# Edge loop of a four-layer GNN on one core: the sum, maximum and product of the group ahead placed between the one-hots of the two item chains

## The reference, cut to what matters

```
g      = leaky_relu(xl[src] + xr[dst] + edge_attr @ W_e, 0.2)
logits = einsum('ehc,hc->eh', g, att)
amax   = segment_max(logits, dst);  ex = exp(logits - amax[dst])
out    = segment_sum(xl[src] * ex / (segment_sum(ex, dst)[dst] + 1e-16), dst) + bias
```

## Time and profile before

| | |
|---|---|
| median of 3 runs | 6465.83 us |
| profiled execution, its own time | 6478.12 us |
| its span | 6476.2 us |
| mean granted TensorE clock | 0.731 |
| PE, DVE, ACT, POOL busy, share of the span | 78%, 46%, 28%, 60% |
| first and last start of a gather of the edge loop | 438.3 and 2843.4 us |

### The profile page before, as it was taken

The page is one execution under the profiler, slowest core; times in us unless marked ns, Lnnn a source line. Parts: engine busy times, 40 slices in busy tenths (PEclk is TensorE's granted clock), DMA queues, the critical chain, the costliest instruction groups (busy, mean ns, idle before and its releaser), DMA issues. The chain is left out here.

```text
span 6476.2 us, 113947 instructions
## 1 busy us (share of the span) xinstructions
PE 5047.6 (78%) x35178; PEld 4313.9 (67%) x35178; DVE 2978.9 (46%) x3937; ACT 1845.2 (28%) x3914; POOL 3856.6 (60%) x3427
## 2 busy tenths in 40 slices
PE   2328888888888888870799967888787788885899
PEld 2315665666555665550799967778777777774899
DVE  7657877777777777755422131111111111112321
ACT  0015555555555455530000002222222222221100
POOL 5747887888888888853000017777777777776000
PEclk9667888888888888865899975555555555555799
DMA  9325555555555555531799946666667666664598
GB/s 358 83 79 141 154 144 148 155 153 144 149 150 152 142 152 153 155 97 36 259 366 366 364 143 215 202 206 201 201 204 208 207 205 204 205 209 122 228 397 329
DMA packets 622991, 1260.53 MB, mean 195 GB/s; under 512 B 131705, under 2 KB 431290, under 8 KB 597220
## 3 DMA queue, kind: packets, MB, share of 16 engines
q10 hardware_dynamic: 217740, 649.85, 31.5%
q1 hardware_dynamic: 295768, 492.49, 21.2%
q0 software_dynamic: 109184, 115.05, 8.6%
HBM read 923.85 MB, written 490.51 MB: 218 GB/s over the span
## 5 line engine op out<-in xcount | busy, mean ns | idle before, releaser
L697 POOL DMA_INDIRECT att_gl<-tab_l,top_zero x1568 | 1928.4, 1230 | 488.5 <-issue 475.6
L1177 POOL DMA_INDIRECT sum_gl<-tab_l,top_zero x1568 | 1547.4, 987 | 517.5 <-issue 477.6
L930 ACT ACTIVATE att_acc<-att_pc 128x392 bf16<-128x392 f32 x2352 | 1088.0, 497 | 1326.7 <-PE att_pc L713 1201.3
L710 PE MATMUL att_pc<-att_ohl,att_ohv 128*128 128x392 bf16 x2352 | 867.5, 369 | 260.9 <-DVE att_ohl L810 260.8
L1105 PE MATMUL sum_pm<-sum_msg,sum_S 128*128 128x64 f32 x3136 | 683.6, 413 | 388.8 <-ACT sum_msg L1145 388.8
L713 PE MATMUL att_pc<-att_acc,att_ohv 128*128 128x392 bf16 x2352 | 861.4, 366 | 116.2 <-ACT att_acc L930 112.7
L1105 PEld LDWEIGHTS sum_pm<-sum_msg,sum_S 128*128 128x128 f32 x3136 | 657.8, 321 | 421.6 <-ACT sum_msg L1145 219.1
L1075 DVE TENSOR_TENSOR sum_t<-sum_pb,sum_gl 128x512 f32<-128x512 f32 x196 | 135.6, 692 | 1659.3 <-DMA sum_gl<-tab_l,top_zero 1276.0
L1087 PE MATMUL sum_pb<-sum_wbs,sum_ea 64*128 64x64 f32 x3136 | 694.5, 419 | 28.1 <-DMA sum_ea<-in_ea64T 28.1
L729 PEld LDWEIGHTS att_pl<-att_xe,att_S 128*128 128x128 f32 x3136 | 603.9, 218 | 161.2 <-issue 138.7
L1087 PEld LDWEIGHTS sum_pb<-sum_wbs,sum_ea 64*128 64x128 f32 x3136 | 676.1, 329 | 39.7 <-DMA sum_ea<-in_ea64T 28.3
(11 more groups left out here) (373 smaller groups left out, 5268.7 us busy)
## 6 DMA issues: line engine op xcount, KB each, us to landing
A<-att_acc SPq DMA_DIRECT2D x2352, 98.0 KB
l_a<-A SPq DMA_DIRECT2D x147, 1568.0 KB, 9.3
att_dall<-in_dst ACTq DMA_DIRECT2D x224, 448.0 KB
sum_dall<-in_dst ACTq DMA_DIRECT2D x196, 512.0 KB, 7.1
hop_at<-AT SPq DMA_DIRECT2D x56, 1568.0 KB
sum_a<-A ACTq DMA_DIRECT2D x49, 1568.0 KB, 10.2
AT<-sum_at ACTq DMA_DIRECT2D x49, 1568.0 KB, 6.4
l_at<-AT SPq DMA_DIRECT2D x42, 1568.0 KB
```

The lines of the kernel that those rows point to most:

```text
L697: nc.gpsimd.indirect_dma_start(out=gl[s][:, k * GQ + j, :], out_offset=None, in_=g.tab_l, in_offset=bass.IndirectOffsetOnAxis(ap=g.ix[:, c ...
L710: nc.tensor.matmul(pc[c][m % 2][:, 0:LO], ohv[c][h][:, m, :, 0], ohl[c][h][:, m // 2, :, m % 2], start=True, stop=False)
L930: nc.scalar.activation(acc[c][n % CR][:, :], pc[c][m % 2][:, 0:LO], ACT.Copy).then_inc(s_acc[c], 1)
L1177: nc.gpsimd.indirect_dma_start(out=gl[n % RB][:, j, :], out_offset=None, in_=g.tab_l, in_offset=bass.IndirectOffsetOnAxis(ap=g.ix[:, c:c + ...
```

## The change

`items` makes ohl ahead of ohv. `logits` keeps its first three operations; the fourth, with the signal `s_L` behind it, becomes `head_sums`. VectorE's slot is then: `same`, `items` of chain 0, softmax or messages where due, `logits` of the group ahead, `items` of chain 1, `head_sums` of the group ahead. No other engine's program changes.

```diff
                     if not known(i, 1) or t >= 2:
                         dve.wait_ge(s_mm[c], i * (CB * CJ) + (at0[t - 1] if t >= 2 else (-SLOTS[SL - 1], 0)[t]))
+                    v.tensor_tensor(ohl[c][h][:, 0:w // 2, :, :], spread(c_lo2[:, :, :].unsqueeze(1), [P, w // 2, LO, 2]),
+                                    spread(g.lo[:, bass.ds(n0, w)].rearrange("p (j two) -> p j two", two=2).unsqueeze(2),
+                                           [P, w // 2, LO, 2]), ALU.is_equal).then_inc(s_oh[c], 1)
                     v.tensor_tensor(ohv[c][h][:, 0:w, :, :], spread(c_row2[:, :, :].unsqueeze(1), [P, w, P, 2]),
                                     spread(g.vals[:, bass.ds(n0, w), :].unsqueeze(2), [P, w, P, 2]), ALU.is_equal)\
                         .then_inc(s_oh[c], 1)
-                    v.tensor_tensor(ohl[c][h][:, 0:w // 2, :, :], spread(c_lo2[:, :, :].unsqueeze(1), [P, w // 2, LO, 2]),
...
                     step(v.tensor_tensor(t2[:, :, :], t2[:, :, :], spread(att[:, :].unsqueeze(1), [P, GQ, D]),
                                          ALU.mult))
+
+                def head_sums(n, b, s, k):
+                    step = InOrder(dve, s_step, n * 3 + (b * 4 + 6))
                     step(v.tensor_reduce(L[s][:, :, k * GQ:(k + 1) * GQ].rearrange("p h g -> p g h"),
...
                         same(i, t)
-                        for c in range(CH):
-                            items(i, t, c)
+                        items(i, t, 0)
                         if k == 1 and known(b, 1):
                             v.memset(apart[:, :], 0.0).then_inc(s_step, 4)
                         elif k == 1:
                             softmax(b - 1, i * SL + (t - 1))
                         if k == 2 and not known(b, 1):
                             messages(b - 1, 1 - s)
+                        n = i * SL + (t - 1)
                         if t:
-                            logits(i, i * SL + (t - 1), b if k else b - 1, s if k else 1 - s, (k - 1) % NQ)
+                            logits(i, n, b if k else b - 1, s if k else 1 - s, (k - 1) % NQ)
                         elif not known(i, 1):
-                            logits(i - 1, i * SL + (-1), b - 1, 1, NQ - 1)
+                            logits(i - 1, n, b - 1, 1, NQ - 1)
+                        items(i, t, 1)
+                        if t or not known(i, 1):
+                            head_sums(n, b if k else b - 1, s if k else 1 - s, (k - 1) % NQ)
 
                 turns(dve, TURNS, turn)
                 logits(TURNS - 1, NBT * NQ - 1, LAST, LAST % R, NQ - 1)
+                head_sums(NBT * NQ - 1, LAST, LAST % R, NQ - 1)
```

More of the change, by code:

```diff
@@ L809, in items @@
                         .then_inc(s_oh[c], 1)
-                    v.tensor_tensor(ohl[c][h][:, 0:w // 2, :, :], spread(c_lo2[:, :, :].unsqueeze(1), [P, w // 2, LO, 2]),
-                                    spread(g.lo[:, bass.ds(n0, w)].rearrange("p (j two) -> p j two", two=2).unsqueeze(2),
-                                           [P, w // 2, LO, 2]), ALU.is_equal).then_inc(s_oh[c], 1)
                 def logits(i, n, b, s, k):
```

## The result

The changed kernel takes 7848.37 us (median of 4 runs, 7844.53 to 7854.08) against 6467.03 us before: ratio 1.2138, 95% interval 1.2117 to 1.2159. It is slower by 1381 us. The forecast was 7850 us, range 7300 to 8180. The profiled execution took 7849.59 us, its span is 7847.7 us.

What follows compares the result with a forecast made beforehand. POOL was taken to bound the edge loop while the other engines' round trip stays under 10.8 us. After the change, PE's groups 92.2, pauses 38.0 and messages 5.5 us a turn, x 28, add 1381: 7850 us, range 7300 to 8180.

Steps and rivals of the forecast that it cites:

- The round trip: Edge loop: logits waits for PE's last expand, PE for chain 1's one-hots queued behind logits, so their work no longer overlaps.
- The pause of 4.37 us: From PE's last expand to chain 1's one-hots: 4.37 us with six items, 3.69 with four, then 0.63 for item (c1, m0).
- The softmax, put at nothing: Slots 1 and 5 on VectorE: its five short steps are done while PE runs its group, so cost nothing.
- Messages, 2.75 us twice a turn: Slots 2 and 6: messages ahead of logits start t1 2.75 us later, 5.5 us a turn.
- PE's groups, 92.2 us a turn: From L722 to the last expand: eight groups at a mix of clocks take 92.2 us a turn.
- a choice between 61 and 106 us: PE's eight groups a turn: 61.2 us if the clock never falls, 105.8 us if it is always low.
- the 6909 of that bound: Whole kernel if the clock holds or returns at once: 6909 us, +443; as a rival, chance 0.12.
- Sum 135.7 us a turn: Edge loop: 92.2 + 38.0 + 5.5 us a turn, x 28 = 3800 us against 2419, +1381.
- The signs: Expected in the profile after: longer PE waits before L710, t1 waiting for PE, POOL waiting on VectorE, loop near 3800 us.
- The swap, costed at nothing: The changed order of the two one-hots within a pair costs nothing, since PE waits for both.
- The rival by POOL: Two short spells of one-hots hold back fewer gathers: 227 us gained, about 6240 us; chance 0.03.
- by that there is nothing to gain here: On the rival by POOL: the skill lets two-SBUF-input tensor_tensor stop only GpSimd's reads; yet a 1.86 us gather was held up.

Runs made afterwards that it cites:

- e6: The changed kernel, VectorE untouched, with all seven expands of a slot on PE right behind the attributes, ahead of chain 1's first item: 6713.08 us.
- v1: The kernel before, unswapped, with chain 0's one-hots made a slot ahead, behind the logits, so that the pairs stand apart: 6327.66 us.
- e4: The changed kernel, with the messages of slots 2 and 6 moved behind chain 1's one-hots and the head sums: 7659.22 us.
- e2b: The changed kernel, with 12 to 16 (slots with messages: 30) useless matmuls added on PE in each pause: 6944.25 us.
- e5: The changed kernel with the swap undone, att_ohv again ahead of att_ohl in each pair: 7856.81 us.
- v1s: The kernel before, with chain 0's one-hots made a slot ahead and att_ohl ahead of att_ohv in each pair: 6321.12 us.
- v3: The kernel before, swapped, with both chains' one-hots made a slot ahead, together behind the logits and ahead of the next same: 6452.68 us.
- v2s: The kernel before, swapped, with the comparison into S (same) between the two pairs of one-hots: 6322.35 us.

## Why the prediction was right

- *The round trip.* Right. PE and VectorE alternate as the timelines of after show; e6 shows that it is the wait and not the distance of the pairs: VectorE's order is that of the changed kernel, and 1135 us come back. v1 sets only `same` between the pairs and says nothing about that distance.
- *The pause of 4.37 us (six items) and 3.69 (four), each with 0.63 for item (c1, m0).* Together 5.00 and 4.32; measured from window to window 5.06 to 5.19 with six items and 4.38 and 4.39 with four (slot 2 to 3 is 2370.78 to 2375.16). In the passage shown, the 0.06 over are the hand-over back to PE (0.06) and 0.11 more before the first one-hot, against a hand-over to t1 of 0.03 instead of 0.15. The softmax, put at nothing, costs nothing: the passages into slots 1 and 5, which have it, take 5.16 and 5.07, those into slots 0 and 4 5.19 and 5.06.
- *Messages, 2.75 us twice a turn.* 7.24 us with four items is 2.85 more than the 4.39 between slots 6 and 7; 7.92 with six is 2.85 more than 5.07. e4 gave 2.96 a time in waits.
- *PE's groups, 92.2 us a turn.* Measured 92.1, term by term 4 x 11.81 became 11.09, 12.40, 11.86, 12.70 (48.05 for 47.24), 9.66 became 9.59, 6.98 became 6.13, 14.17 stayed. Errors of 0.8 and 0.9 cancelled. The rows of groups that had caught the low clock in the kernel before were the right neighbours; that part was a choice between 61 and 106 us, and e2b shows the choice was sound: with the clock kept, the time is 6944 us for the 6909 of that bound.
- *Sum 135.7 us a turn.* Measured 136.5. Over the median 1381 us, for 1381 forecast; so near a hit is luck in the cancelling terms and in the loop's two ends.
- *The signs.* The wait ahead of L710 was forecast at some 800 us and is 1014; my own sum held the latter: 43.5 us a turn less 8 x 0.63 are 38.5, x 28 = 1077, less the item (c0, m0) within each; the 800 was a slip. The wait is also put down to L810, the line at which att_ohv now stands, and not to L807. t1 waits for PE in 163 groups, not in nearly all: in 56 slots VectorE waits at the messages instead, and t1 then follows. From the start of t1 to the end of att_ohv it is 4.34 us (2252.85 to 2257.19) for 4.2. Clock 0.55 to 0.65: 0.65. POOL waits, t1 waits for no gather: right.
- *The swap, costed at nothing.* Right for this change (e5: 8 us) and incomplete as reasoned. I looked only at who waits for the pair. In the loop before, which POOL bounds, it is worth 105 us.
- *The rival by POOL* (fewer gathers held back by shorter spells) names an effect that is real: 1230 to 1137 ns in v1s, 144 us off the time. That it comes of shorter spells is not shown: the swap alone, with the spell as long as before, gives most of it, and v3 loses it again. It was rightly kept out of this change by its own condition, since PE's group and the pause together exceeded 10.8 us; in the changed kernel the mean gather is 1071 ns and POOL is idle for 2080 us. The sentence "by that there is nothing to gain here" went too far: each gather takes its row numbers from an SBUF tile (`g.ix`), so a stop of GpSimd's reads alone could hold it up. Which part of it is held no run shows.

Of the clock: the low level is 1.2 GHz, the high one 2.4. Slot 7 of the earlier trace rows and slots 3 and 7 of after run at 0.50 to their ends, with PE busy throughout. The Trainium skill, "TensorE: Matmul & The Clock Gate", "HAM oscillation — how this bites in real kernels", describes a kernel in which waits inside a loop bring the low clock back in every pass; the windows of after and e2b agree.

## What to carry to other kernels

Before an operation is moved ahead of another in a stream, follow its wait once round: if the engine that it waits for is itself held by what is now queued behind it, the two engines stop overlapping, and the time of the turn becomes their sum. A pause on TensorE is to be priced twice, as itself (477 us here, by e2b) and as the clock that it costs (904 us), the second from groups of the same kernel that met the low clock. To set two things apart in a stream, move work between them that waits for nothing that they hold up, as `same` here. Making one of them a round ahead can be the same stream written otherwise (v1s and v2s): compare the order round the loop before counting it as a second version.

## What the runs showed of the hardware

- Useless matmuls in pauses that exist anyway took the granted clock of the loop from 0.65 to 1.00 and the kernel from 7848 to 6944 us.
- Gathers issued by GpSimd are held up while VectorE runs comparisons: 0.94 us alone, 1.85 when one starts early in a 1.38 us 16-bit att_ohl, 1.48 on the mean of 208 beside the 32-bit comparison into S alone (v3). The order of two 16-bit comparisons with no dependence between them moved the mean of 1568 gathers from 1230 to 1152 ns.
- The changed loop repeats itself: two turns in a row, counted from slot 4's L722, are 136.55 and 136.51 us (starts 2121.33, 2257.88, 2394.39). The granted clock falls and rises at the same places: the turn from 2461.14 has 0.69, 0.69, 0.77, 0.50, 0.63, 0.65, 0.79 and 0.50 in slots 0 to 7, as the one shown.
